# A two-layer network on one core: the second layer's convolution taps move from TensorE to VectorE, its centring to GpSimd, and its end is edited

## The reference, cut to what matters

```
xn = layernorm(x)
x  = x + state_space(xn) + feed_forward(xn)
```

```
z, x_ssm, B, C, dt_raw = split(n @ in_proj)            # 256, 256, 128, 128, 4 columns
x_conv = silu(conv_b + sum_k shift(x_ssm, 3 - k) * conv_w[:, k])    # k = 0..3, causal, per channel
dt = softplus(dt_raw + dt_bias);  h_t = h_(t-1) * exp(-exp(A_log) * dt_t) + (dt_t * x_conv_t) B_t
y_t = h_t C_t + D * x_conv_t;   out = (y * silu(z)) @ out_proj
```

## Time and profile before

| what | us |
|---|---|
| median of 3 runs | 635.24 (633.25 to 636.52) |
| the profiled execution | 637.8 |
| its span, first to last instruction | 636.0 |
| TensorE busy | 587.0 (92%) |
| VectorE busy | 384.4 (60%) |
| ScalarE busy | 455.0 (72%) |
| GpSimd busy | 142.9 (22%) |

### The profile page before, as it was taken

How to read it: one execution, slowest core, us unless ns; L and a number is a source line. 1 busy time by engine, 2 the same in 40 slices (tenths; PEclk the granted TensorE clock), 3 DMA queues, 4 the chain that set the end, 5 groups by cost and what they waited for, 6 DMA issues and landing times.

```text
span 636.0 us, 11391 instructions
## 1 busy us (share of the span) xinstructions
PE 587.0 (92%) x4063; PEld 346.6 (54%) x4063; DVE 384.4 (60%) x1044; ACT 455.0 (72%) x608; POOL 142.9 (22%) x172
## 2 busy tenths in 40 slices
PE   4669999999999999999897899799989999999997
PEld 3324334444343334333334487378768888887886
DVE  7885855546444353475416764777576576675854
ACT  2368997999989999888666365556757575666672
POOL 2043222020110021103600745102013131323131
PEclk9779999999999999999989999999999999999999
DMA  7112002013422220300317220200000000000000
GB/s 225 30 34 68 2 2 68 0 40 109 162 101 101 85 83 1 102 34 14 103 26 222 66 76 38 76 2 0 1 0 2 2 18 0 2 18 1 18 2 16
DMA packets 31159, 31.00 MB, mean 49 GB/s; under 512 B 6896, under 2 KB 21008, under 8 KB 31104
## 3 DMA queue, kind: packets, MB, share of 16 engines
q1 hardware_dynamic: 29856, 27.71, 14.0%
q0 software_dynamic: 1248, 2.57, 1.1%
HBM read 13.44 MB, written 12.89 MB: 41 GB/s over the span
## 4 chain that ended last, share of the span: by engine, by line
PE 63%; DVE 19%; ACT 6%; issue 6%; POOL 2%; DMA 2%; SPq 2%; DVEq 0%; POOLq 0%; ACTq 0%
PE ps L1319 18%; PE ps L1300 8%; PE ps L92 5%; PE ps L94 4%; PE ps L93 4%; PE ps L1626 2%; PE ps L1396 2%; PE ps L1383 2%; PE ps L1212 1%; DVE r L2469 1%; DVE r L2401 1%; PE ps L1496 1%; DVE r L2398 1%; SPq L713 1%; PE ps L1388 1%
## 5 line engine op out<-in xcount | busy, mean ns | idle before, releaser
L959 ACT ACTIVATE r<-ps 128x1024 f32<-128x1024 f32 x272 | 258.3, 1034 | 36.3 <-PE ps L1300 32.7
L1319 PE MATMUL ps<-r 128*32 128x512 f32 (+3 forms) x1280 | 148.7, 551 | 2.2 <-DVE r L2041 0.9
L839 POOL TENSOR_SCALAR_AFFINE_SELECT r<-r 128x512 f32<-128x512 f32 (+1 forms) x80 | 46.9, 589 | 221.4 <-ACT r L959 221.3
L1300 PE MATMUL ps<-r2r 32*128 32x512 f32 (+3 forms) x640 | 79.2, 453 | 8.6 <-DMA r2r<-r2r 4.5
L1300 PEld LDWEIGHTS ps<-r2r 32*128 32x128 f32 x640 | 34.5, 184 | 51.2 <-issue 22.7
L877 POOL TENSOR_TENSOR r<-r 128x512 f32<-128x512 f32 x16 | 23.4, 1462 | 134.8 <-ACT r L1137 134.8
L1319 PEld LDWEIGHTS ps<-r 128*32 128x32 f32 x1280 | 27.9, 109 | 42.8 <-issue 30.4
L94 PE MATMUL ps<-r2r 128*128 128x512 f32 x112 | 44.2, 395 | 0.0
L93 PE MATMUL ps<-r2r 128*128 128x512 f32 (+1 forms) x96 | 35.8, 373 | 0.0
L817 POOL DMA_INDIRECT rows_by_expert<-r x16 | 17.7, 1109 | 63.5 <-DVE r L1956 59.6
L1137 ACT ACTIVATE r<-r 128x512 f32<-128x512 f32 x16 | 10.1, 632 | 30.3 <-DVE r L2469 30.3
(11 more groups left out here) (408 smaller groups left out, 1240.2 us busy)
## 6 DMA issues: line engine op xcount, KB each, us to landing
rows_by_expert<-r SPq DMA_DIRECT2D x34, 258.0 KB, 2.5
r2r<-r2r SPq DMA_DIRECT2D x60, 64.0 KB, 2.0
r<-in_f_W SPq DMA_DIRECT2D x1, 2048.0 KB, 9.4
r<-rows_by_expert SPq DMA_DIRECT2D x23, 64.5 KB, 1.9
res<-in_x SPq DMA_DIRECT2D x4, 256.0 KB, 4.5
r<-in_g_h1T SPq DMA_DIRECT2D x1, 1024.0 KB, 5.6
r<-in_g_h2T SPq DMA_DIRECT2D x1, 1024.0 KB, 7.8
r<-rows_by_token SPq DMA_DIRECT2D x4, 256.0 KB, 3.9
```

The costliest lines, as they stand in the source:

```text
L839: pool.affine_select(blk, blk, pattern, ALU.is_ge, nothing, base=0, channel_multiplier=-1).then_inc(s_msk, 1)
L959: act.activation(probs[:, n % PBUFS, :, :], ps[:, b:b + 2, :], ACT.Exp).then_inc(s_exp, 1)
L1300: m = pe.matmul(ps[:, 2 * (n % SBUFS) + h, at:at + TB - query], kst[32 * j:32 * j + 32, group, P * kt:P * kt + P], qst[32 * j:32 * j + 32, ...
L1319: m = pe.matmul(ps[32 * j:32 * j + 32, 6, query:TB], vp[:, kt, group, :], probs[:, (2 * v + j // 2) % PBUFS, j % 2, at:at + TB - query], s ...
```

## The change

1. A c unit becomes one product, three matmuls: the raw projection. ScalarE copies it to `xc` (`taken`), makes `conv_b + w3 * x` (`last_tap`), VectorE adds the other three taps (`taps_added`), ScalarE takes the tanh (`sums_tanh`), VectorE gates (`gated_c`, now per half). GpSimd copies three columns at each block's edge. For block 0 this is in the projection stage, for blocks 1 to 3 in the feed-forward stage of the block before. The preparation of tap-scaled weights goes.
2. The unit order `PROJ` changes; `normalised` is cut in two, and `measured(q + 1)` stands ahead of `xs_low(q)`.
3. Centring and the low part of the feed-forward weight `fh1` move to GpSimd.
4. The scale `w3_s` is multiplied into the weights f3; DOWN is added to `res` in one operation.
5. Chunk 0 has no product with the zero state; the last chunk updates no state. The last tile's DOWN and its projected product are summed in one PSUM bank, and its 128 rows are written by a DMA of their own.

```diff
+        PROJ = ([("XS", 0)] + early(0) + [("XS", 1)] + late(0)[2:] + early(1) + [("XS", 2)] + late(0)[:2] + late(1)[2:]
+                + early(2) + [("XS", 3)] + late(2)[2:] + early(3) + [("T", 0)] + late(1)[:2] + late(3)[2:] + [("T", 1)]
+                + late(2)[:2] + late(3)[:2] + [("T", 2), ("T", 3), ("A", 0)])
...
 @@ sync
+                n = TPB if b < NB - 1 else TPB - 1
+                sp.dma_start(out[TB * b:TB * b + P * n, :].rearrange("(i p) d -> p i d", p=P),
+                             res[:, TPB * b:TPB * b + n, :]).then_inc(s_out, 16)
+            sp.wait_ge(s_fin, NB + 1)
+            sp.dma_start(out[T - P:T, :], res[:, NT - 1, :]).then_inc(s_out, 16)
...
 @@ gpsimd
+            pool.memset(xc[:, :, 0, 0:HALO], 0.0).then_inc(s_halo, 1)
+            pool.wait_ge(s_fhi, FO + 2)
+            for k in range(FO):
+                pool.tensor_tensor(fh1l[:, k, :], fh1[:, k, :], fh1h[:, k, :], ALU.subtract).then_inc(s_fh1, 1)
             for b in range(NB):
+                pool.wait_ge(s_inv, b + 1)
+                for t in range(TPB * b, TPB * b + TPB):
+                    pool.tensor_scalar(xn[:, t, :], res[:, t, :], mv[:, t, 0:1], inverse[:, b, 0, t % TPB:t % TPB + 1],
+                                       ALU.subtract, ALU.mult).then_inc(s_xn2, 1)
                 pool.wait_ge(s_xn2, TPB * (b + 1))
+                pool.wait_ge(s_xs, TPB * (b + 1))
...
+            for b in range(NB - 1):
+                pool.wait_ge(s_cvr, 2 * (b + 1))
+                pool.tensor_copy(xc[:, :, b + 1, 0:HALO], xc[:, :, b, TB:TB + HALO]).then_inc(s_halo, 1)
...
 @@ scalar
+            def taken(b):
                 for m in range(MI):
                     act.wait_ge(s_pj, proj_done(f"c{m}", b))
+                    act.activation(xc[:, m, b, HALO:], ps[:, proj_bank(f"c{m}", b), :], ACT.Copy).then_inc(s_cvr, 1)
+            def last_tap(b, m):
+                act.wait_ge(s_convw, 16)
+                act.wait_ge(s_cvr, 2 * b + m + 1)
+                if b == 1:
+                    act.wait_ge(s_fu, FO)
+                elif b:
+                    act.wait_ge(s_xc, 2 * (b - 1) + m + 1)
+                act.activation(conv_sums(b, m), xc[:, m, b, HALO:], ACT.Identity, bias=convb[:, m:m + 1],
+                               scale=convw[:, m, KW - 1:KW]).then_inc(s_cva, 1)
+            def sums_tanh(b, m):
+                act.wait_ge(s_cvt, 2 * b + m + 1)
+                if b:
+                    act.wait_ge(s_pj, len(PROJ))
+                    act.wait_ge(s_xc, 2 * b + m)
+                act.activation(conv_tanh(b, m), conv_sums(b, m), ACT.Tanh, scale=0.5).then_inc(s_xth, 1)
...
+            roots_of(0)
+            xs_high(0)
+            for b in range(1, NB):
                 roots_of(b)
+                if b >= 2:
+                    taken(b - 2)
+                tokens_read(b - 1)
+                states_read(b - 1)
                 xs_high(b)
             z_tanh(0)
+            taken(2)
+            for m in range(MI):
+                last_tap(0, m)
             tokens_read(3)
             states_read(3)
             xn_high(0)
             z_tanh(1)
+            for m in range(MI):
+                sums_tanh(0, m)
+            taken(3)
             xn_high(1)
             z_tanh(2)
+            z_tanh(3)
...
+                    if o == 0 and b < NB - 1:
+                        last_tap(b + 1, 0)
+                        last_tap(b + 1, 1)
                     middle_gelu(b, o)
+                    if o == 2 and b < NB - 1:
+                        sums_tanh(b + 1, 0)
...
                     last_gelu(b, o)
                     if b < NB - 1:
+                        if o == 0:
+                            sums_tanh(b + 1, 1)
                         up_tanh(b + 1, o)
...
 @@ tensor
+                    joined = TPB * b + i == NCH - 1
+                    dst = ps[:, 3, 0:D] if joined else ps[:, ffn_bank("DOWN", b, 0), P * i:P * i + P]
...
+                if b == NB - 1:
+                    pe.wait_ge(s_cg, NCH)
+                    for m_ in range(MI):
+                        m = pe.matmul(dst, yg[:, (NCH - 1) % 2, m_, :], owT[:, m_, :], start=False, stop=(m_ == MI - 1))
...
 @@ vector
+            def taps_added(b, ms=range(MI)):
+                dve.wait_ge(s_convw, 16)
+                dve.wait_ge(s_halo, b + 1)
+                last = {}
+                for k in range(KW - 1):
+                    for m in ms:
+                        if k:
+                            dve.wait_ge(s_v, last[m])
+                        else:
+                            dve.wait_ge(s_cva, 2 * b + m + 1)
+                        sums = conv_sums(b, m)
+                        added = dve.scalar_tensor_tensor(sums, xc[:, m, b, k:k + TB], convw[:, m, k:k + 1], sums,
+                                                         ALU.mult, ALU.add)
+                        if k < KW - 2:
+                            last[m] = step.mark(added)
+                        else:
+                            added.then_inc(s_cvt, 1)
+            def gated_c(b, m):
+                dve.wait_ge(s_xth, 2 * b + m + 1)
+                if b < NB - 1:
+                    dve.wait_ge(s_halo, b + 2)
+                dve.scalar_tensor_tensor(xc[:, m, b, HALO:], conv_tanh(b, m), 1.0, conv_sums(b, m), ALU.add, ALU.mult
+                                         ).then_inc(s_xc, 1)
...
+            measured(0)
+            normalised(0)
+            for q in range(1, NB):
+                measured(q)
+                xs_low(q - 1)
                 normalised(q)
+            xs_low(3)
             gated_z(0)
+            taps_added(0)
+            xn_low(0)
+            gated_z(1)
             dve.wait_ge(s_pja, act_read("D1", NB - 1))
             step.alone(dve.tensor_tensor(du, btd[:, :, P:P + NH], along(dtb, NT), ALU.add))
             dve.scalar_tensor_tensor(dl, du, -1.0, du, ALU.mult, ALU.min).then_inc(s_dta, 1)
+            for m in range(MI):
+                gated_c(0, m)
             xn_low(1)
             gated_z(2)
+            gated_z(3)
...
                     elif b < NB - 1:
                         gated_low(b + 1, o - FO - 1)
+                    if b < NB - 1 and o in (1, 3):
+                        taps_added(b + 1, (o // 2,))
+                    if b < NB - 1 and o in (3, 5):
+                        gated_c(b + 1, o // 2 - 1)
...
             down_added(NB - 1)
+            dve.sem_inc(s_fin, 1)
+            dve.wait_ge(s_f4, NB + 1)
+            dve.tensor_tensor(res[:, NT - 1, :], res[:, NT - 1, :], ps[:, 3, 0:D],
+                              ALU.add).then_inc(s_fin, 1)
```

## The result

The kernel after took 644.95 us (median of 4 runs, 643.31 to 647.62) against 635.88 (633.25 to 638.21) for the kernel before beside it: ratio 1.0136, 95% interval 1.0100 to 1.0173. Slower, as forecast, but by 9.1 us where 3.5 were forecast, and 0.95 above the top of the range. A second set on another chip gave 1.0150 (1.0119 to 1.0181). The profiled execution took 647.62, its span is 645.9.

What follows compares the result with a forecast made beforehand. In the feed-forward stage it took TensorE and the chain over VectorE, ScalarE and GpSimd as equally late. Before the layer -0.3, projection -10.0, taps +15.9, end -2.1 make +3.5; median 635.24 becomes 638.7 us, range 625 to 644.

Steps and rivals of the forecast that it cites:

- Its own signs: Right: first gated product near 446, blocks 0 to 2 of 46 to 48 us; wrong: no TensorE wait above 1, start past 450.
- Feed-forward taps: Later blocks' convolution in the feed-forward stage delays TensorE at three hand-overs a block: +15.9 us, bounds 0 and 23.8.
- (a): Hand-over to chunk 5's decays, slack nil: taps and gelu delay less shorter down_added, +1.8 us a block, +2.65 in block 0.
- (b): Behind middle_low(2): taps and gated c delay chunk 6's decays and the product freeing UP(2, 1)'s bank, +2.7 us a block.
- (c): Gated product at o = 5, in the hand-over to chunk 7's decays: +0.5 us a block.
- Projection stage: First gated product of the feed-forward stage moves from 456.35 to 446.35: -10.0 us, at least 6 and at most 16.8 saved.
- GpSimd's new work: Subtractions, centrings and additions take 19 to 31 us on GpSimd, hidden; only L2343 is held, at most 1.3 us a block.
- the walk: Projection stage followed operation by operation: D0 from 410.08 to 411.9, ScalarE late from 427, first gated product at 446.35.
- Centring's price: GpSimd's 16 centrings in the projection stage at 0.54 us each, above 1.30, hidden at both ends.
- 3 and 4: Port lock stretches the first part, +3 us, chance 0.12; TensorE's clock falls in new gaps, +5 us, chance 0.04.
- Rivals 1 and 2: Taps fall into idle time partly (629.6, chance 0.20) or wholly (621.5, 0.10); TensorE's full 16.8 us return (631.9, 0.07).
- The end, and before the layer: Last chunk and last tile shortened, -2.1 us (bounds -1.0, -2.6); tap preparation dropped before the layer, -0.3 (0, -1.5).

Runs made afterwards that it cites:

- e3: The kernel after without the convolution of blocks 1 to 3 in the feed-forward stage, that computation left out; ratio to the kernel before 0.9880.
- e1: The kernel after with more dummy matmuls on TensorE in three of its waits of the first part; ratio to the kernel before 1.0126.
- e15: The kernel after with GpSimd's four fh1 subtractions moved behind the convolution's edges, centring staying early on GpSimd; ratio to the kernel before 1.0089.
- e2: The kernel after with the four fh1 subtractions and 16 centrings back on VectorE; ratio to the kernel before 1.0154.
- e8: The kernel after with GpSimd's subtractions, centring and residual additions held until VectorE wrote the last normalised tile; ratio to the kernel before 1.0241.
- e16: e14 with centring and the fh1 subtractions on GpSimd, placed as in e15, instead of on VectorE; 621.19 us, ratio to the kernel before 0.9852.
- e11: e5 with centring and the fh1 subtractions back on VectorE, GpSimd copying edges between its second and third residual additions; ratio to the kernel before 0.9984.
- e13: e11 with the later blocks' tap operations and gated products spread nearly one by one, ScalarE's last taps moved too; ratio to the kernel before 0.9879.
- e14: e13 with more dummy matmuls on TensorE in two waits of the first part; 621.89 us, ratio to the kernel before 0.9847.
- e12: The kernel after with ScalarE's part of the later blocks' convolution kept and VectorE's left out of the computation; ratio to the kernel before 0.9912.
- e5: The kernel after with the later blocks' convolution at other places of the same stage, all work kept; 630.82 us, ratio to the kernel before 1.0010.
- after_again: The kernel after, unchanged, measured a second time on another chip; 639.92 us, ratio to the kernel before 1.0150.
- e4: The kernel before with only the end's edits (w3's scale, joined addition, first and last chunk cut, last tile joined); 629.10 against 630.64 us, ratio 0.9978.

## Why the prediction was wrong, step by step

**Its own signs.** The waits came, above the 1 us that it had set. Blocks 0 to 2 of 50.0, 48.4 and 49.3 us lie above its 46 to 48, and the first gated product at 450.28 is later than the 450 that it had named as a sign of being wrong.

**Feed-forward taps: right in kind, 2.3 short.** Forecast +15.9, measured 18.2 (-0.9 +19.1). Its three places are the waits that the trace shows, and e3 ties all of it to the later blocks' convolution. Split by the distances of the states (state(4) to (5), (5) to (6) and (6) to (7) in block 1): (a) 2.96, 2.36 and 2.36 (block 0 less the 0.94 of the earlier state(0)) against 2.65, 1.8, 1.8; (b) 2.9, 2.8, 3.1 against 2.7; (c) 0.3, 0.3, 1.0 against 0.5. The mis-sized term is (a), "the shorter `down_added` ... gives 0.72 back": middle_low(0) waited 0.91 for ScalarE, whose gelu stood behind two last taps of 0.8 each, so VectorE had nothing to give back: against state(4), middle_low(0) came 0.15 later than before, not 0.32 earlier. My 0.4 for the gelu's delay and the 0.72 should have been one comparison of two engines and not two terms. Some 0.9 us of (b) and (c) in block 2 go with a fall of the clock (0.59 over 588 to 592 us, behind a wait of 2.17); e1 and e15 have such a fall and the longer block in block 1, and not in block 2.

**Projection stage: the step that failed.** Forecast -10.3 with what lies before, measured -6.1. Two things failed in it.

The first is "**GpSimd's new work**": "In the first part only L2343 reads two tiles, at most 1.3 a block". None of after's four L2342 (the L2343 of before) was held (0.68), because none began while a two-tile operation of GpSimd ran; in e1 one did and took 1.75. Held were VectorE's TENSOR_SCALARs, which read one tile of SBUF and write SBUF, by GpSimd's two-tile operations (1.02 for 0.17, 2.43 for 1.12). e15, e2 and e8 show it: rows to the first low half 6.2, 6.0 and 6.0 instead of 8.2. In rows to gated this is 2.2 us where the clock fell in neither (e1 43.36, e16 41.14) and 2.3 in e15 against after.

The second is the clock, which the walk left at 1.00: 2.9 us in the kernel after (46.30, and 43.36 in e1), 2.9 in e15 against e16. The new order alone was enough for a fall: in e15, e11 and e13 nothing held VectorE ahead of D0, and the clock fell behind waits of 0.3 to 0.4 and 1.6 to 1.7 us (0.29 and 0.55 in the kernel before), though not in e2 with the same waits. The walk had this delay of D0 (410.08 to 411.9) and priced it as its length. With both gone the stage gives 40.97 (e14) and 41.14 (e16); the walk had given 446.35 - 404.37 = 41.98. So the walk itself held to 1 us, ScalarE's chain from 427 us on with it.

In the prediction I cited the Trainium skill, "SBUF — State Buffer", section "SBUF: two separate sides", for the operation with two SBUF inputs. That sentence names a second taker of the lock, a VectorE operation in a 2-port performance mode, and I left it out. The section "Who interferes with whom" of the same page of the Trainium skill counts `tensor_scalar` among the operations that can run in such a mode; the trace agrees (1.02 instead of 0.17). VectorE's batch-norm statistics read one tile too and were not held: 0.87 beside L868 and 0.87 in the kernel before. The first of these two sections of the Trainium skill also says that any GpSimd operation can hold the pair; here the one-input centring held single VectorE operations by 0.12 us at most (1.18 for 1.12, 0.28 for 0.16 on a 128x4 one), and the rows' addition not at all (0.68).

**Centring's price.** I took 0.54 from the nearest row, bounds to 1.30; it was 0.87 to 0.94 (3.46 to 3.76 for four). It was hidden, as said: T(0) waited 1.28 us for ScalarE.

**Rivals.** 3 and 4 both came true in part, at other places than I gave them: not L2343, and not only the waits of 2.2 us in the feed-forward stage (0.9 us) but 1.49 and 0.83 in the first part. Rounds of 6.00, 5.07 and 6.79 us were above the 4.9 that rival 3 had set. I had priced each alone, and let speak against 4: clock 1.00 with TensorE busy 6.8 of 10. That row held for its own pattern of gaps. Rivals 1 and 2 fell: nothing was swallowed, and TensorE waited for ScalarE at T(0) and for VectorE at z(3) (1.74).

**The end, and before the layer.** -2.1 forecast, -2.2 measured; -0.3 forecast, -0.4 measured in one profile. That agreement is luck: the rows' arrival itself differs by up to 5 us between kernels alike up to there (395.6 in e1, 401.0 in e12).

**Sum.** In the profiles +9.9 against +3.5: 4.2 from the projection stage and what lies before, 2.3 from the taps, -0.1 from the end.

## What to carry to other kernels

When work goes to GpSimd, list every operation of VectorE beside it, TENSOR_SCALARs with one input within SBUF too, and keep GpSimd's two-input operations out of a stretch where VectorE feeds TensorE; a one-input operation was nearly free beside single VectorE operations. An idle stretch of VectorE is room for two-input operations only if GpSimd is idle in it as well: the later blocks' convolution cost 18.1 us at its first places (6.2 + 5.5 + 6.4 over the blocks of before, block 0 less its 0.94), 9.3 in e5 with the taps still in runs of three, and 3.6 in e13 with them nearly one at a time (2.0 + 0.8 + 0.8). ScalarE's operations moved as well in both, and no run divides these gains between the engines. And where TensorE waits already, a new gap can cost more than its length: here the clock fell and took 1.9 to 2.9 us more.

## What the runs showed of the hardware

- GpSimd's two-input 128x512 operation held VectorE's one-input TENSOR_SCALARs within SBUF until it ended: a 128x4 one took 1.02 us instead of 0.17 in the kernel after and in e1, where the fh1 subtractions ran beside it, and 0.17 in e2, e8 and e15, where they didn't. It did not hold the batch-norm statistics (0.87 beside it and 0.87 alone).
- GpSimd's one-input 128x128 operation held single VectorE operations by 0.12 us at most. Beside six chained tap operations both engines became slower: in e8 these took 4.84 us instead of after's 4.06, and four centrings 5.24 instead of 3.12:

```profile
426.11 4.84 DVE L2389 SCALAR_TENSOR_TENSOR r<-r,row 128x512 f32<-128x512 f32 x6 [0.98 <-ACT r L1087]
```

```profile
426.98 5.24 POOL L870 TENSOR_SCALAR xn<-res,small 128x128 f32<-128x128 f32 x4
```

- TensorE's clock in the first part fell to 0.50 in the profiles of after, after_again, e3, e5, e11, e12, e13 and e15, and for a shorter stretch in e8. It stayed at 1.00 in e2, whose code and whose gaps of 0.29 and 1.59 us are e11's, and in e4, whose first part is that of before. In the three with more dummy matmuls (e1, e14, e16) it never fell there, though e1 kept one wait of 1.47 us. What a fall cost, in rows to gated, went from 1.9 us (e3 and e12 against e1) to 2.9 (after against e1, e15 against e16). Why it spared e2 is open.
- e14 (621.89 us against 630.86) and e16 (621.19 against 630.89), the best versions, do all the work of the kernel after, with more on VectorE or in TensorE's dummies.
